# A DLRM tower on one core: group 0 worked in two parts, the start-up loads reordered, the adds three tiles behind, and a last layer in row strips

## What is computed

```python
e = stack([tbl_f[ids[:, f]] for f in range(39)], axis=1)          # (512, 39, 16), float32
def cin(X0, Xi, W, b):                                            # W: (128, 39 * Fi)
    return einsum('hjk,bjd,bkd->bhd', W.reshape(128, 39, Fi), X0, Xi) + b
X1 = cin(e, e, W0, b0); X2 = cin(e, X1, W1, b1); X3 = cin(e, X2, W2, b2)
z  = concat([X1.sum(2), X2.sum(2), X3.sum(2)], axis=1)            # (512, 384)
h  = relu(concat([z, dense_ctx], 1) @ W_top1 + b_top1)            # 400 -> 512
h  = relu(h @ W_top2 + b_top2)                                    # 512 -> 256
y  = h @ W_top3                                                   # 256 -> 1
```

## Time and profile before

| | |
|---|---|
| median of 3 runs | 673.1 us |
| the profiled execution | 672.67 us, of which 670.6 us are the span from its first to its last instruction |
| granted TensorE clock | 0.995 of full |
| busy | PE 641.9, DVE 521.2, ACT 488.3, POOL 361.1 us |
| group 0 begins on PE | 44.37 us |
| group 1 begins on PE | 79.71 us |
| last chunk ends, about | 612.3 us |

### The profile page before, as it was taken

One profiled execution on the slowest core, in us unless ns is written; L12 is line 12 of the kernel. 1 busy time (PEld: TensorE's weight loads), 2 busy tenths in 40 slices (PEclk: granted clock), 3 DMA queues, 4 the chain that ended last, 5 costly groups with the idle time before them and its releaser, 6 DMA issues.

```text
span 670.6 us, 11899 instructions
## 1 busy us (share of the span) xinstructions
PE 641.9 (96%) x2516; PEld 461.4 (69%) x2516; DVE 521.2 (78%) x1478; ACT 488.3 (73%) x1692; POOL 361.1 (54%) x308
## 2 busy tenths in 40 slices
PE   0689999999999999999999999999999999999998
PEld 0246777777777777777777777777777777785483
DVE  0346888878888888888888878888888888897590
ACT  1137877778787868787877878787868787897293
POOL 6878766575656565755666675656575221121000
PEclk9799999999999999999999999999999999999999
DMA  6457687767676777667667767676777657567100
GB/s 225 60 92 168 112 183 133 173 131 162 124 160 128 159 150 163 142 134 155 139 144 134 167 130 161 124 160 129 160 150 162 142 102 178 126 122 215 31 1 0
DMA packets 61944, 91.05 MB, mean 136 GB/s; under 512 B 34599, under 2 KB 38548, under 8 KB 61671
## 3 DMA queue, kind: packets, MB, share of 16 engines
q0 software_dynamic: 14192, 51.02, 42.0%
q1 hardware_dynamic: 47734, 39.85, 21.2%
HBM read 10.59 MB, written 1.28 MB: 18 GB/s over the span
## 4 chain that ended last, share of the span: by engine, by line
PE 91%; POOL 3%; DMA 3%; issue 2%; SPq 1%; ACT 0%; DVE 0%; ACTq 0%; POOLq 0%
PE t_bank L426 22%; PE t_bank L427 21%; PE t_bank L428 21%; PE x_bank L394 14%; PE small_bank L411 5%; POOL emb L324 3%; PE t_bank L491 1%; PE t_bank L471 1%; PE t_bank L502 1%; PE t_bank L503 1%; PE t_bank L514 1%; PE t_bank L505 1%; DMA emb<-in_table,idx 1%; PE x0t_bank L402 1%; DMA emb_scratch<-emb 1%
## 5 line engine op out<-in xcount | busy, mean ns | idle before, releaser
L567 ACT ACTIVATE prod<-t_bank,x0t 128x128 f32<-128x128 f32 x1472 | 417.5, 377 | 114.6 <-PE t_bank L428 109.3
L671 DVE SCALAR_TENSOR_TENSOR prod<-t_bank,x0t,prod 128x128 f32<-128x128 f32 x1024 | 287.9, 343 | 80.1 <-PE t_bank L428 75.8
L426 PE MATMUL t_bank<-w_hi,x_hi 128*128 128x512 f32 (+1 forms) x640 | 307.5, 480 | 0.6 <-DVE x_lo L660 0.3
L427 PE MATMUL t_bank<-w_lo,x_hi 128*128 128x512 f32 (+1 forms) x640 | 247.8, 387 | 0.0
L428 PE MATMUL t_bank<-w_hi,x_lo 128*128 128x512 f32 (+1 forms) x640 | 247.0, 386 | 0.0
L324 POOL DMA_INDIRECT emb<-in_table,idx x160 | 211.8, 1324 | 48.5 <-issue 46.8
L334 POOL TENSOR_TENSOR diag<-x0t,mask 128x320 f32<-128x320 f32 x64 | 87.8, 1372 | 195.4 <-DVE prod L671 97.7
L426 PEld LDWEIGHTS t_bank<-w_hi,x_hi 128*128 128x128 f32 x640 | 120.2, 188 | 54.7 <-issue 29.7
L427 PEld LDWEIGHTS t_bank<-w_lo,x_hi 128*128 128x128 f32 x640 | 120.5, 188 | 47.1 <-issue 25.3
L428 PEld LDWEIGHTS t_bank<-w_hi,x_lo 128*128 128x128 f32 x640 | 120.1, 188 | 24.2
L703 DVE TENSOR_TENSOR prod<-prod 128x768 f32<-128x768 f32 (+2 forms) x192 | 117.4, 611 | 6.0 <-DMA prod<-prod 5.7
(11 more groups left out here) (73 smaller groups left out, 242.8 us busy)
## 6 DMA issues: line engine op xcount, KB each, us to landing
prod<-prod POOLq DMA_DIRECT2D x63, 768.0 KB, 7.1
shared<-rep SPq DMA_DIRECT2D x96, 234.0 KB
shared<-rep SPq DMA_DIRECT2D x48, 78.0 KB
emb<-in_table,idx POOLq DMA_INDIRECT x160
G<-in_w SPq DMA_DIRECT2D x1, 2496.0 KB
rep<-rep SPq DMA_DIRECT2D x28, 78.0 KB
rep<-emb_scratch SPq DMA_DIRECT2D x20, 78.0 KB
prod<-in_w SPq DMA_DIRECT2D x1, 1536.0 KB, 7.1
```

What stands on the lines that cost most here:

```text
L426: pe.matmul(acc, hi, w1_hi[:, cols], start=True, stop=False)
L427: pe.matmul(acc, hi, w1_lo[:, cols], start=False, stop=False)
L567: last = act.activation(prod[:, s, SLOT[c] + u, :], t_bank[c % T_BANKS][:, u * H:(u + 1) * H], ACT.Copy, scale=x0t[:, s, j:j + 1])
L671: last = dve.scalar_tensor_tensor(unit, t_bank[c % T_BANKS][:, u * H:(u + 1) * H], x0t[:, s, j:j + 1], unit, ALU.mult, ALU.add)
```

## The change

Group 0 is worked in two **parts** of 16 samples (256 columns, two tiles). Each has its own ids (four DMAs), its own index and five gathers (126 and 124 partitions, each row of ten folded into two of five), its own two stores (of 63 and of 62 partitions), four loads, and factors (three DMAs for the first and one for each second factor, 256 columns). Part 0's seven pair products are 256 columns wide and go into `t_bank[3]` before the main loop; part 1's are done inside group 0, after chunks 10 to 16. The pair products of group 1 move to chunks 23, 25, ... 35 of group 0. Part 0's second factors are issued by SP and ACT by turns and have buffers of their own.

SP's queue begins with eight loads of ids and starts for the parts, then those of the whole, the pair weights, and the first 20 of 39 fields of W1 (two pieces). The other two pieces come behind the copies of part 0. The eleven constants are issued by ACT. W1 is split into hi and lo piece by piece; PE waits for the pieces at chunks 0, 3, 5 and 7 of the first tile.

`BEHIND` is 3 and `G_AT` 0: the sums of tile t are done in tile t + 3 and its product after chunk 0 of tile t + 4. In the last tile DVE does two tiles' sums; the slot folded on DVE is summed first, the other behind it. The four `dense` products of the first layer take 16 rows each, now at partitions 0, 32, 64 and 96, and stand behind the product of the last tile but one; one `first_layer` of `G` moves behind the thirty triples.

```diff
-BEHIND = 2
+BEHIND = 3
+PARTS = 2
+W1_PIECES = [(0, 12), (12, 20), (20, 28), (28, F)]
+W1_EARLY = 2
+W1_CHUNKS = (0, 3, 5, 7)
+PART_X0T_AT = 8
+PART_FORM_AT = [7 + b for b in range(BLOCKS)]
+PART_PAIR_AT = [10 + b for b in range(BLOCKS)]
+FIRST_X0T_AT = 20
+FIRST_FORM_AT = [21 + 2 * b for b in range(BLOCKS)]
+FIRST_PAIR_AT = [p + 2 for p in FIRST_FORM_AT]
+FIRST_GATHERS = [(0, 5), (5, 10), (10, 10), (10, 10)]
-G_AT = 2
+G_AT = 0
...
 @block.sync
+            for part in range(PARTS):
+                load_part_ids(part)
             sp.dma_start(ids_all[:, :], ids).then_inc(ids_loaded, 16)
             sp.dma_start(table_at[:, :], starts).then_inc(ids_loaded, 16)
-            sp.dma_start(pair_a_raw, pair_a).then_inc(w_loaded, 16)
-            sp.dma_start(pair_b_raw, pair_b).then_inc(w_loaded, 16)
-            sp.dma_start(w1_raw, w1).then_inc(w_loaded, 16)
...
+            sp.dma_start(pair_a_raw, pair_a).then_inc(pair_w_loaded, 16)
+            sp.dma_start(pair_b_raw, pair_b).then_inc(pair_w_loaded, 16)
+            for i in range(W1_EARLY):
+                load_w1(i)
...
+            def store_part(part):
+                sp.wait_ge(part_gathered[part], 16 * PART_GATHERS)
+                begin, n = PART_BEGIN[part], PART_SIZE[part]
+                row = PART_GATHERS * D
+                for fold in range(FOLDS):
+                    sp.dma_start(emb_dram[begin:begin + n, fold * row:(fold + 1) * row],
+                                 part_emb[fold * n:(fold + 1) * n, part, :]).then_inc(part_stored[part], 16)
+            def load_part(part):
+                sp.wait_ge(part_stored[part], 16 * FOLDS)
...
+            def factors_of_part(part):
+                sp.wait_ge((early_x0_loaded, x0_loaded)[part], 16 * X0_LOADS)
...
+                if part > 0:
+                    sp.wait_ge(early_pair_ready, BLOCKS)
+                for b in range(1, BLOCKS):
+                    if part > 0 or b % 2 == 1:
+                        sp.dma_start(part_second_at(part, b), rep[b:b + PAIRS, 0, cols]).then_inc(part_second[b - 1], 16)
-            x0_of(0, 0, at_once=True)
-            factors(0, 0)
+            store_part(0)
+            load_part(0)
+            factors_of_part(0)
+            for i in range(W1_EARLY, len(W1_PIECES)):
+                load_w1(i)
+            store_part(1)
+            load_part(1)
+            factors_of_part(1)
             x0_of(1, 1, at_once=True)
...
 @block.gpsimd
-            for g in range(AHEAD):
-                index(g, g)
-                for i in range(GATHERS):
-                    gather(i, g)
+            for part in range(PARTS):
+                gather_part(part)
+            pool.wait_ge(ids_loaded, 16 * 2)
+            index(1, 1)
+            for i in range(GATHERS):
+                gather(i, 1)
...
 @block.tensor
+                if first_tile and c in W1_CHUNKS:
+                    pe.wait_ge(w_split_lo, W1_CHUNKS.index(c) + 1)
...
-            transpose_x0(0, True)
+            pe.wait_ge(early_x0_loaded, 16 * X0_LOADS)
+            transpose_x0(0, range(PART_TILES), early_x0t_mm)
             for b in range(BLOCKS):
-                pair_product(0, b)
+                part_pair_product(b)
-            pe.wait_ge(w_split_lo, 1)
             group(0, 0, first=True)
...
             for m in range(M1):
                 if m == 2:
+                    g_product(TILES - 3, 1)
                     pe.wait_ge(act_scaled, TILES * NA)
                     pe.wait_ge(dve_scaled, TILES * ND)
-                if m == M1 - 1:
-                    g_product(TILES - 2, 2)
-                first_layer(m, P, 0, z0[:, :], start=True)
-                first_layer(m, D, 3, dense[:, :])
-            g_product(TILES - 1, 3)
+                first_layer(m, 0, z0[:, :], start=True)
+            pe.wait_ge(diag_ready, TILES)
+            g_product(TILES - 2, 3)
+            for m in range(M1):
+                strip = slice(m * STRIP, m * STRIP + D)
+                pe.matmul(h1_bank[m][:, :], wt1[strip, 3, m * P:(m + 1) * P], dense[strip, :],
+                          start=False, stop=False, tile_position=(m * STRIP, 0))
+            g_product(TILES - 1, 2)
...
-            for m in range(M1):
-                first_layer(m, P, 1, G[:, F, :])
+            for m in range(M1 - 1):
+                first_layer(m, 1, G[:, F, :])
...
+            first_layer(M1 - 1, 1, G[:, F, :])
             pe.wait_ge(z2_ready, 1)
...
 @block.scalar
...
+            for i in range(W1_EARLY):
+                split_w1_hi(i)
+            act.wait_ge(early_x0_loaded, 16 * X0_LOADS)
+            for b in range(2, BLOCKS, 2):
+                act.dma_start(part_second_at(0, b), rep[b:b + PAIRS, 0, part_cols(0)]).then_inc(part_second[b - 1], 16)
+            for s in range(PART_TILES):
+                copy_x0t(0, s, first=True)
+            split_w1_hi(W1_EARLY)
+            part_x1_hi()
             group(0, first=True)
...
 @block.vector
+            for b in range(BLOCKS):
+                form_part_pairs(0, b)
+            split_w1_lo(W1_EARLY)
+            split_part_x1_lo()
...
             group(GROUPS - 1, 1, last=True)
-            for i in range(RED):
-                sum_over_j(TILES - 2, GROUPS - 1, 2, i)
             fold_last(TILES - 1, 3)
             for i in range(RED):
-                sum_over_j(TILES - 1, GROUPS - 1, 3, i, by_dve=True)
+                sum_over_j(TILES - 2, GROUPS - 1, 3, i, by_dve=True)
+            for i in range(RED):
+                sum_over_j(TILES - 1, GROUPS - 1, 2, i)
```

More of the change, by code:

```diff
@@ L224, in _, with load_part_ids @@
         def _(sp):
+            def load_part_ids(part):
+                begin, n = PART_BEGIN[part], PART_SIZE[part]
+                for to, src in ((part_ids, ids), (part_at, starts)):
+                    for fold in range(FOLDS):
+                        sp.dma_start(to[fold * n:(fold + 1) * n, part, :],
+                                     src[begin:begin + n, fold * PART_GATHERS:(fold + 1) * PART_GATHERS]).then_inc(part_ids_loaded[part], 16)
+            for part in range(PARTS):
+                load_part_ids(part)
@@ L370, in group @@
                         fold((s - 1) % TILES_PER_GROUP)
-                    if gathers and s < INDEX_TILE:
+                    if first:
+                        for i in range(*FIRST_GATHERS[s]):
+                            gather(i, half)
+                    elif gathers and s < INDEX_TILE:
                         for i in range(GATHERS_EARLY, GATHERS):
@@ L578, in group @@
                         if c == 0:
-                            if s > 0 and not last:
-                                copy_x0t(g + 1, s - 1, False)
-                            if s == 0 and not first:
-                                copy_x0t(g, TILES_PER_GROUP - 1, False)
+                            if first:
+                                if s == 1:
+                                    for tile in range(PART_TILES, TILES_PER_GROUP):
+                                        copy_x0t(0, tile, first=True)
+                                if s == 3:
+                                    for tile in range(TILES_PER_GROUP - 1):
+                                        copy_x0t(1, tile)
+                            else:
+                                if s > 0 and not last:
+                                    copy_x0t(g + 1, s - 1)
+                                if s == 0:
+                                    copy_x0t(g, TILES_PER_GROUP - 1)
@@ new lines, in group @@
+                            if last and s == TILES_PER_GROUP - 1:
+                                slot = i // 2
+                                for half_of_it in range(2):
+                                    sum_over_j(t - BEHIND + slot, g, slot, 2 * (i % 2) + half_of_it)
+                            else:
+                                sum_over_j(t - BEHIND, g if s >= BEHIND else g - 1, (s - BEHIND) % TILES_PER_GROUP, i)
+            dve.wait_ge(pair_w_loaded, 16 * 2)
+            dve.tensor_tensor(w_pair[:, :], pair_a_raw, pair_b_raw, ALU.add).then_inc(w_pair_ready, 1)
```

294 lines of the change are left out of this document (213 added, 81 removed).

## The result

The changed kernel takes 680.8 us (median of 4 runs, 680.59 to 683.16), the kernel before 673.2 (4 runs, 672.78 to 676.59): ratio 1.0106, 95% interval 1.0076 to 1.0136. It is **slower by 1.1%**, clear of no change by its interval, where 667.0 (663.0 to 671.5) was forecast. The profiled run took 680.76 us, its span is 679.0.

What follows compares the result with a forecast made beforehand. PE, busy 96% of the span, was taken to bound the kernel, leaving start and end to win. 672.67 profiled less 4.5 (group 1 earlier) and 1.6 (end) gives 666.6; with 0.4 for the median 667.0, range 663.0 to 671.5.

Steps and rivals of the forecast that it cites:

- the thin cover: Loop: DVE's last add ends 0.6 us before chunk 0 at the tightest of four turns; nothing lost.
- the feed eats more: Rival, group 0: part 1 and group 1 in series on SP, four us more, 671.0; chance 0.17.
- the feed line inside group 0, from 27.4 to 52.8: SP's queue from part 0's copies issued (27.4) through part 1's stores, loads and copies to group 1 in `rep` (52.8).
- Part 0 lands at 15.0: Start: part 0's fifth gather lands between 13.8 and 17.0, taken as 15.0.
- First chunk 33.0: Start: PE's first chunk at 33.0 (31.5 to 35.5), 11.4 us earlier.
- Part 1's stores landed by 32.7: Group 0: W1's 1.25 MB flow until about 31.4, part 1's stores behind them in SP's queue end at 32.7.
- Group 1's load 5.4: SP's queue in group 0: loads behind group 1's store take 5.4 us, more beside a fold; in `rep` at 52.8.
- Group 1 begins at 75.2: End of group 0: group 1 begins at 75.2, before 79.71, 4.5 us gained.
- End 1.6 won: Behind the last chunk: 0.75 us ahead of W2 and 0.86 from the moved `first_layer`; gain 2.6 to loss 1.5.
- Holds better: Rival, group 0's feed: gathers land at 13.8, half-size transfers scale, line 3 to 4 us shorter, 663.5; chance 0.13.
- strips in sequence: Rival, the end: strips run one behind the other, 3.1 us more between the last two `g_product`, 669.5; chance 0.08.
- Slower: Rival, loop: DVE's last add over 0.6 us later stalls each group; at 1.2 us later, 680; chance 0.05.

Runs made afterwards that it cites:

- experiment 2: The changed kernel with ACT's eleven constants held until part 0's ids are there; 680.1 us, ratio 1.0100.
- 13: The changed kernel with all of W1 ahead of part 0's store and ACT's constants held until part 0's ids have landed; 680.7 us, ratio 1.0106.
- 14: The changed kernel with all W1 ahead, constants held for part 0's ids, and group 1's store ahead of part 1's factors; 677.3 us, ratio 1.0062.
- experiment 10: The changed kernel with all four pieces of W1 issued ahead of part 0's store; 677.5 us, ratio 1.0062.
- Experiment 4: The changed kernel with POOL's first fold held until group 1's rows are in `rep`; 686.7 us, ratio 1.0180.
- Experiment 1: The kernel before with only the loop and end parts of the change, its own start kept; 675.5 us, ratio 1.0026.
- experiment 9: The changed kernel's start, with adds two tiles behind and the strips and end as in the kernel before; 690.2 us, ratio 1.0247.
- experiment 8: The kernel before with only the dense products in four row strips; 673.0 us, ratio 0.9997.
- experiment 5: The kernel before with the change's loop and end parts, group 1's pair products formed at every second chunk of group 0; 672.4 us, ratio 0.9982.

## Why the prediction was wrong, point by point

**Right.** PE bounds the loop; a loop group stayed at 36.0, the thin cover costing nothing there by itself. The strips ran side by side in 1.1 us. The moved `first_layer` is hidden. DVE's adds set the end, and they brought W2's first product 1.64 us closer (forecast 0.75). The direction of "the feed eats more" was right, "four us more on that line", at three times its size.

**The step that failed: the feed line inside group 0, from 27.4 to 52.8.** Its terms, forecast against measured:

- *Part 0 lands at 15.0*: 18.64. "At some 0.35 us of issue each the first gather moves to about 4.7": it left at 8.69. ACT now issues constants beside SP, and the ids landed 4.7 us later for it (experiment 2). I had costed that move at nothing. Yet it isn't the cause of the loss: with ids early the rows still landed at 16.4 to 18.0 (experiments 2, 13 and 14). Reading as gathers that wait for weights was wrong too, or at least not enough: see experiment 2.
- *First chunk 33.0*: 36.65. 2.3 us of this are part 0 in `rep` (23.86 for 21.6), 1.4 the copies and products behind it.
- *Part 1's stores landed by 32.7*: 37.17. I had W1's 1.25 MB done at 31.4 and a store of 1.3 behind it. The store took 7.3, and 3.4 without W1 beside it (experiment 10). Here the Trainium skill was weighed too lightly ("DMA: Bandwidth & Descriptors", Why a DMA increments its semaphore by 16 and not by 1): a DMA over 62 partitions uses two engines, one over 63 nine. Part 0's stores of 63 partitions took 1.75, part 1's of 62 took 3.4 with no weights beside them. That agrees in direction; but part 1's had the last copies of part 0 beside them, and no run changed the partitions alone.
- *Group 1's load 5.4, "more where a fold runs: in rep at 52.8"*: 60.02. Of the 7.2 us, 3.5 to 4.3 are the later issue (50.6 for 46.3 to 47.1, which is 44.1 and a store of 2.2 to 3) and the rest the fold (9.4 us for the 5.7 to 6.5 that 52.8 leaves). The fold was named and given 0.3 to 1.1 us of that. Experiment 4 shows the price, and that this way of waiting did not avoid it.
- *Group 1 begins at 75.2*: 86.15, the stalls of 9.4 us in place of 5.3, on a start 3.7 us later, and a clock of 0.93 for 1.00, which no step had; PE stood still when it fell.
- *Nothing lost in group 1*: 1.6 lost, its factors under a fold.
- *End 1.6 won*: 0.8. The gain ahead of W2 was larger than forecast, and 1.7 us went to a lower clock in the nine products. No step had it.

**The rivals.** "Holds better" and "strips in sequence" are out. "The feed eats more" is what happened: 11 us, not 4. "Slower" was told for the wrong place: not every group stalls at its tightest turn; one group does, when the next group's factors meet a fold and the last add stands behind DVE's wait for them. The two rivals are one mechanism seen from two sides. Experiment 1 shows it with the old start too: 4.6 us lost in group 1, in the part of the change that was counted as a gain. With the chance of slower at 0.05 the forecast was far too sure: each step of the line from ids to group 1 was taken near its best case, though they are in series.

**Where the gain of two parts went.** Half the bytes were to halve the line. But the line did not scale with them: with all weights ahead, half a group is in `rep` at 27.1 to 27.9, when a whole one was before. What sets that time (the 3.3 MB of weights, the first gather packets at 10 us, the number of transfers) no run took apart. With half of the weights behind, the other half pays. And all that part 1 needs is put into SP's line ahead of group 1, whose x0 was in `rep` at 49.29 before and at 60.02 after.

## What to carry to other kernels

When a first group is cut in two to start sooner, work out when the *next* group's data arrives, with every transfer added ahead of it at its contended time; what counts is that line, not the first chunk. Stores and loads of small packets paid for most large transfers beside them (weights, folds), whichever queue issued these, and moving the large one mostly changed who paid. A kernel whose loop looks free of stalls can sit 1 us from one: compare issue times of neighbouring transfers with the kernel before, not only the idle time.

## What the runs showed of the hardware that I had not expected

- While ACT and SP both issue small DMAs, one issue on SP took 3.67 us (4.10 above), against 0.31 where ACT held back (experiment 2), and ids of a few KB landed 6.2 us after issue.
- Gathers issued at 3.95 to 9.4 landed at 17.6, those issued at 8.69 to 14.15 at 18.6: issuing 4.7 us sooner gained 1.0. No gather packet was moved before 9.4 us in any of ten profiles, also where the first gather had left at 3.9; then they came through beside the weights.
- A fold of 768 KB beside a load of 4 DMAs to `rep` made 5.25 us into 9.4 (into 6.7 in experiment 10); beside first factors, 5.6 into 8.1 to 9.1.
- DVE's branch back to the head of its loop took 3.5 to 4.2 us in experiment 9 and 0.2 to 0.3 in every other kernel.
- Four fp32 products of 16 rows in row strips of 32 ran fully side by side: 1.1 us for all, against 1.12 for one.
- In the stretch of W2's nine products the granted clock fell in 10 of 13 profiles of the new end with strips, and in one of three of the old order (experiment 9, not before and not experiment 8). PE's idle time in the eight microseconds ahead was 2.3 us in experiment 1 and 2.3 in experiment 5, and the clock held in the one and fell in the other; what decides is open.
